# A four-layer transformer kernel whose steps are written out in one order, with the inverse root of one layer formed on VectorE

## The chip, the cores and the metric

The kernel runs on one core of a Trainium2 chip. The metric is device time in microseconds. Three runs of the kernel before took 1157.16, 1159.32 and 1162.14 us; the median is 1159.32 us. Five engines work side by side, each through its own list of instructions in a fixed order: TensorE (PE, with its weight loads as PEld), VectorE (DVE), ScalarE (ACT), GpSimd (POOL) and SyncE (SP, which here only issues DMAs). Semaphores order them.

## The reference

The input is x, 4 batches of 512 tokens of 256 numbers, and a condition vector for each batch. Four layers follow one another; every layer works on the whole of x, and batches never mix.

```python
# layer 0: one head, rmsnorm and film, softmax attention, MLP with exact gelu
h = film(rmsnorm(x)); Q, K, V = h@q_w, h@k_w, h@v_w
x = x + softmax(Q@K.T * 256**-0.5) @ V @ proj_w;  x = x + gelu(film(rmsnorm(x))@w1) @ w2
# layer 1: 16 heads of 16, layernorm, cosine attention: q and k are scaled to length 1
q = q / max(sqrt(sum(q*q)), 1e-12) * exp(min(scale_mul, log 100));  k = k / max(sqrt(sum(k*k)), 1e-12)
x = x + gamma1 * proj(softmax(q@k.T) @ v);  x = x + gamma2 * mlp(ln(x))
# layer 2: 16 heads, layernorm, softmax(q@k.T / 4), gates, MLP
# layer 3: 16 heads, softmax(q@k.T) / 16, no MLP; output = norm(h1) + h1
```

## The kernel before

One batch of one layer is a *job*; there are 16 jobs, 0 to 15. A job of layers 1 to 3 has 4 *units* of 4 heads, and a unit has 16 score steps (4 token blocks of 128 by 4 heads). Work is cut into some 2,400 *steps*, and the list `PLAN` holds them in one order. Every engine walks the whole list and does its own share of each step, so the list sets the order on each engine, on SP's DMA queue too; nothing is reordered at run time. The steps that the prediction speaks of:

- `scores` (L701): a 64-row matmul whose 128x512 result lands in one bank of PSUM; ACT reads it with an exponential into `probs` (L908 one bank, L905 two banks in one instruction, where two scores of layer 1 stand next to each other in the list and their banks too). Two such matmuls use the upper and the lower 64 rows of the array and run side by side.
- `max` (L676), in layers 2 and 3 alone: the same product of another unit the other way round; DVE reduces it to a row maximum (L1231). In layer 1 `gmax` (L684, read by DVE at L1211) gives a bound in its place.
- `av` (L714): four matmuls with 32 columns each, `probs` times V, into a bank of their own (`AVB`).
- Dense products (L602, L603, L604: three fp32r products for one exact one) for q, k, v, proj, fc1 and fc2; `oT1`, `oT2`, `hT1` and `hT2` are transposes.
- The results of all these but `av` go round a ring of 7 banks (`RING = 7`). A matmul that claims a bank waits until the reader of its last use but six is done (`claim`).
- In layer 1 `qktok` puts q and k, token by token, into `qk`; `qkss` squares (ACT) and sums (DVE, L1162); `qkroot` clamps the sums (DVE, L1167) and takes the root (ACT, L878); `qkrs` takes the reciprocal (DVE, L1171) and scales (L1173); `qknorm` multiplies (DVE, L1180); `q` and `k` then transpose `qk` (PE, L664).

`PLAN` is computed. Tables such as `COSINE` and `FFN` give steps a time in ticks (a tick is four score steps), and sorting by these gives the order in layer 0. In layers 1 to 3 the score and maximum steps stand in pairs, and for each two ticks a pattern says how they mix with the rest: in `"p6 A p8 0 p4 1"` six steps of scores and maxima come, then two `av` (`A`), eight more, the other steps of the first tick, four, and those of the second tick. All windows of a layer share eight patterns.

Of the kernel before, what the change touches and what calls it, by code (L numbers as in the profile page):

```python
# [6 lines left out]
F32R = mybir.dt.float32r  # L7
ALU = mybir.AluOpType
# [5 lines left out]
P = 128  # L14
# [13 lines left out]
EPS = (1e-6, 1e-6, 1e-5, 1e-5)  # L28
SCALE = (DIM ** -0.5, 1.0, HD ** -0.5, 1.0)
# [27 lines left out]
def direct(j):  # L57
# [29 lines left out]
LEAD_IN = {"stat1": (-24.09,), "norm1": (-23.23,), "hT1": (-14.74, -14.56), "qktok": (-12.53, -12.04, -11.51, -10.52),
           "qkss": (-12.22, -11.69, -11.15, -10.36), "qkroot": (-10.28,), "v": (-7.19, -7.01), "qkrs": (-9.94,),
           "qknorm": (-9.71, -9.63, -9.35, -9.17), "q": (-8.33, -7.97), "k": (-8.15, -7.79),
           "stack": (-7.03, -6.95, -0.36, 1.0),  # L90
           "gmax": (-5.39, -5.21, -5.03, -4.85, -4.67, -4.49, -3.6, -3.42, -2.52, -2.34, -2.16, -1.98, -1.8, -1.62, -1.44, -1.26),
           "shift1": (-0.98, -0.98), "crow": (-0.9, 0.28, 1.7, 1.7)}
COSINE = {"hT1": (-15.95, -15.04), "qktok": (-13.9, -13.8, -12.05, -11.4), "qkss": (-12.9, -12.7, -11.9, -10.95),
          "qkroot": (-10.5,), "v": (-10.95, -9.2), "qkrs": (-10.15,), "qknorm": (-9.85, -9.8, -9.65, -9.6),
          "q": (-8.9, -8.4), "k": (-8.8, -8.2), "stack": (-7.3, -6.0, -2.65, 0.6), "stat1": (-18.0,), "norm1": (-17.2,),
          "gmax": (-7.9, -7.89, -7.4, -7.39, -6.9, -6.89, -6.4, -6.39, -5.9, -5.89, -5.4, -5.39, -4.9, -4.89, -4.4, -4.39),
          "shift1": (-4.0, -4.0), "crow": (-2.99, -2.5, -1.05, 1.95)}
QKV = {"hT1": (-18.7, -14.34), "q": (-12.95, -10.7), "k": (-12.7, -10.05), "v": (-8.75, -5.2),
       "stack": (-8.25, -7.85, -2.25, 0.45), "stat1": (-22.35,), "norm1": (-20.3,)}
ATTN = {"oT1": (17.1, 17.56, 17.57, 17.83), "oT2": (18.45, 18.71), "proj": (19.2, 19.85), "stat2": (20.7,),  # L100
        "norm2": (22.55,)}
FFN = {"hT2": (23.5, 23.91), "fc1": (25.6, 25.81, 25.82, 25.83, 29.55, 29.56, 29.57, 29.58), "gelu": (25.84, 29.59),
       "fc2a": (27.45, 29.55), "fc2": (30.55, 31.2)}
FFN3 = {"hT2": (23.3, 23.76), "fc1": (25.6, 25.61, 25.72, 25.73, 29.65, 29.66, 29.67, 29.68), "gelu": (25.74, 29.69),
        "fc2a": (26.65, 27.9), "fc2": (31.15, 31.55)}
OUTPUT = {"gatefix": (20.05,), "final": (23.3, 25.45, 26.35, 31.45), "store": (27.25, 30.85, 30.95, 33.7),
          "bias": (18.35,)}
LAST = {"bias": (-0.3,), "gatefix": (14.5,), "oT1": (17.45, 17.96, 18.17, 18.48), "oT2": (19.1, 19.31),
        "proj": (19.45, 19.95), "base": (20.55, 26.35), "stat2": (20.7,), "centre": (21.65, 22.05, 24.65, 25.95),
        "final": (23.25, 26.75, 27.2, 30.2), "store": (19.6, 22.35, 22.95, 24.05)}  # L110
FOR_LAYER = {"gate": (7.7,), "gateout": (10.9,), "gatecast": (11.15, 28.25, 44.35, 56.55), "load_rows": (15.4,),
             "load_mod": (12.45, 33.55), "modrow": (29.75, 46.4), "mod": (30.95, 47.05), "load_gate": (50.6,),
             "load_qkv": (40.9, 43.2, 44.85), "split_qkv": (43.55, 45.3, 50.1), "load_wp": (7.0,), "split_wp": (8.3,),
             "load_w1": (9.9, 11.9, 17.9, 19.35), "split_w1": (10.7, 12.7, 18.7, 20.3),
             "load_w2": (13.9, 16.35, 22.15, 22.5), "split_w2": (14.45, 17.6, 23.55, 25.05)}
FOR_LAST = {"gate": (7.7,), "gateout": (11.45,), "gatecast": (14.75, 26.2, 45.15, 58.65), "load_rows": (14.7,),
            "load_wp": (2.1,), "split_wp": (4.35,), "vones": (-14.55, 3.95)}
# [18 lines left out]
def timed(table, j):  # L136

    return [(TICKS * j + at, (kind, UNITS * j + i, 0) if kind in ("stack", "crow") else (kind, j, i))
            for kind, times in table.items() for i, at in enumerate(times)]


def around(j):

# [1349 lines left out]
```

## Time and profile before

| | busy us | share of the span | instructions |
|---|---|---|---|
| PE | 1085.3 | 94% | 6697 |
| DVE | 702.5 | 61% | 1479 |
| ACT | 794.0 | 69% | 1331 |
| POOL | 490.3 | 42% | 446 |

The profiled execution took 1158.51 us; its span, from the first to the last instruction, is 1156.7 us, and the mean granted clock of TensorE is 0.985. Ends of matmuls are modelled: PE counts as busy while a matmul is in its pipeline, so a slower sequence of matmuls can show as a busy engine. The time from the start of one matmul to the start of the next tells more than the busy share. The chain of waits puts 72% of the span on PE, 9% on DVE, 8% on ACT and 4% on POOL.

### The profile page before, as it was taken

How to read it: one execution, taken by the hardware profiler on the slowest of the kernel's cores; microseconds unless marked ns; L12 is line 12 of the kernel's file. 1: busy time of each engine (PE TensorE's matmuls, PEld its weight loads, DVE VectorE, ACT ScalarE, POOL GpSimd, SP SyncE). 2: the span in 40 equal slices, each digit the busy share in tenths (PEclk: the TensorE clock that was granted, in tenths of full speed). 3: DMA queues.
4: the chain of work that ended last, by engine and by line, in shares of the span. 5: the costliest groups of instructions: out<-in, count | busy, mean ns of one | idle time of the engine just before them, and what ended most of it. 6: DMA issues, size and time to landing. Idle time of an engine off the chain costs nothing.

```text
span 1156.7 us, 19632 instructions
## 1 busy us (share of the span) xinstructions
PE 1085.3 (94%) x6697; PEld 706.0 (61%) x6697; DVE 702.5 (61%) x1479; ACT 794.0 (69%) x1331; POOL 490.3 (42%) x446
## 2 busy tenths in 40 slices
PE   8799989789899999999999999999999999999985
PEld 5577878555565656656657566666656566555442
DVE  6554446545264364234864865865865856898974
ACT  3563655477888678796686686687686787686763
POOL 2553642613633633654335453244344345254122
PEclk9999999999999999999999999999999999999998
DMA  7000001213303203221132231032121211232301
GB/s 234 18 29 28 1 20 38 52 31 101 88 28 95 54 2 90 75 64 29 28 84 65 69 102 38 2 83 65 41 71 29 52 42 52 55 84 56 84 12 36
DMA packets 36385, 64.45 MB, mean 56 GB/s; under 512 B 7208, under 2 KB 22312, under 8 KB 36288
## 3 DMA queue, kind: packets, MB, share of 16 engines
q1 hardware_dynamic: 36288, 63.20, 20.6%
q8 instruction: 56, 0.92, 0.3%
q14 instruction: 41, 0.34, 0.1%
HBM read 22.90 MB, written 2.12 MB: 22 GB/s over the span
## 4 chain that ended last, share of the span: by engine, by line
PE 72%; DVE 9%; ACT 8%; issue 5%; POOL 4%; DMA 1%; SPq 0%; POOLq 0%; DVEq 0%; ACTq 0%
PE AVB L714 13%; PE rings L602 13%; PE rings L604 11%; PE rings L603 11%; PE rings L701 10%; PE rings L676 6%; DVE m L1231 2%; ACT probs L908 2%; PE rings L754 2%; PE rings L749 2%; PE rings L645 2%; POOL gT_l L1334 1%; ACT L908 1%; PE rings L766 1%; POOL tok L1355 1%
## 5 line engine op out<-in xcount | busy, mean ns | idle before, releaser
L1231 DVE TENSOR_REDUCE m<-rings 128x1 fp32r<-128x512 f32 x512 | 319.1, 682 | 101.6 <-PE rings L676 78.4
L908 ACT ACTIVATE probs<-rings 128x512 f32<-128x512 f32 x570 | 297.3, 617 | 96.0 <-PE rings L676 84.5
L701 PE MATMUL rings<-SQ,SK 64*128 64x512 f32 x768 | 236.3, 440 | 12.5 <-ACT probs L905 4.7
L676 PE MATMUL rings<-SK,SQ 63*128 63x512 f32 x512 | 200.9, 459 | 5.4 <-ACT probs L908 4.2
L714 PE MATMUL AVB<-probs,V 128*32 128x512 f32 x1536 | 192.9, 609 | 0.6 <-issue 0.4
L701 PEld LDWEIGHTS rings<-SQ,SK 64*128 64x128 f32 x768 | 107.9, 185 | 139.1 <-issue 52.6
L1334 POOL TENSOR_TENSOR gT_l<-gT_f,gT_h 128x512 fp32r<-128x512 f32 x96 | 121.1, 1282 | 73.9 <-ACT gT_h L968 71.9
L905 ACT ACTIVATE probs<-rings 128x1024 f32<-128x1024 f32 x99 | 97.4, 1035 | 35.9 <-PE rings L701 21.9
L602 PE MATMUL rings<-w_h,gT_h 128*128 128x256 f32 x384 | 111.3, 290 | 2.8 <-POOL gT_l L1334 2.0
L676 PEld LDWEIGHTS rings<-SK,SQ 63*128 63x128 f32 x512 | 84.5, 185 | 39.6 <-ACT probs L908 33.0
L603 PE MATMUL rings<-w_l,gT_h 128*128 128x256 f32 x384 | 107.6, 280 | 0.0
L604 PE MATMUL rings<-w_h,gT_l 128*128 128x256 f32 x384 | 107.5, 280 | 0.0
L968 ACT ACTIVATE gT_f<-rings,colv 128x512 f32<-128x512 f32 x96 | 66.8, 696 | 30.1 <-PE rings L604 27.3
L714 PEld LDWEIGHTS AVB<-probs,V 128*32 128x32 f32 x1536 | 39.9, 110 | 75.8 <-issue 61.7
L602 PEld LDWEIGHTS rings<-w_h,gT_h 128*128 128x128 f32 x384 | 73.2, 191 | 14.1 <-issue 7.6
L602 PE MATMUL rings<-postT_h,w_h 128*128 128x512 f32 x192 | 78.2, 407 | 3.6 <-ACT gT_h L968 2.4
L1329 POOL TENSOR_TENSOR postT_l<-postT_f,postT_h 128x512 fp32r<-128x512 f32 x24 | 32.1, 1337 | 112.7 <-ACT postT_h L844 112.3
L1368 POOL TENSOR_TENSOR tmp<-tmp,gates 128x512 f32<-128x512 f32 x32 | 41.1, 1284 | 88.3 <-DVE tmp L1298 47.0
L604 PE MATMUL rings<-postT_h,w_l 128*128 128x512 f32 x192 | 75.4, 393 | 0.0
L603 PE MATMUL rings<-postT_l,w_h 128*128 128x512 f32 x192 | 75.3, 392 | 0.0
L1298 DVE TENSOR_TENSOR tmp<-rings,rowp 128x512 f32<-128x512 f32 x40 | 27.5, 688 | 78.4 <-PE rings L604 78.4
L1329 POOL TENSOR_TENSOR hT_l<-hT_f,hT_h 128x512 fp32r<-128x512 f32 x30 | 38.7, 1293 | 85.3 <-ACT hT_h L844 85.1
(190 smaller groups left out, 2188.6 us busy)
## 6 DMA issues: line engine op xcount, KB each, us to landing
SQ<-qh SPq DMA_DIRECT2D x96, 128.0 KB, 2.6
SK<-kh SPq DMA_DIRECT2D x96, 128.0 KB, 2.8
SQ<-ql SPq DMA_DIRECT2D x48, 128.0 KB, 2.7
SK<-kl SPq DMA_DIRECT2D x48, 128.0 KB, 2.9
raw<-in_w SPq DMA_DIRECT2D x20, 256.0 KB, 2.7
wmod_s<-in_wmod SPq DMA_DIRECT2D x6, 512.0 KB, 4.2
gates<-gate_rows SPq DMA_DIRECT2D x12, 256.0 KB, 3.4
raw<-in_wqkv SPq DMA_DIRECT2D x9, 256.0 KB, 2.7
```

Of the source, the lines that this page charges most:

```text
L602: pe.matmul(out, sh, mh, start=first, stop=False)
L603: pe.matmul(out, sh, ml, start=False, stop=False)
L604: return pe.matmul(out, sl, mh, start=False, stop=last)
L676: mm = pe.matmul(o[:, :], SQ[a % 4][r:r + KS, n // 2, c * P:(c + 1) * P], SK[a % 4][r:r + KS, n // 2, :], start=True, stop=True)
L701: mm = pe.matmul(o[:, :], SK[a % 4][r:r + KS + 1, n // 2, c * P:(c + 1) * P], SQ[a % 4][r:r + KS + 1, n // 2, :], start=True, stop=True)
L714: mm = pe.matmul(AVB[32 * n:32 * n + 32, :], V[j % 2][:, i, (HD + 1) * h:(HD + 1) * h + 32], probs[:, (4 * t + n) % PROBS, :], start=(i == ...
L905: act.activation(probs[:, n % PROBS:n % PROBS + 2, :], two_banks(kind, a, i), ACT.Exp, scale=SCALE[layer(unit_job(a))]).then_inc(done["sco ...
L908: act.activation(probs[:, n % PROBS, :], bank(kind, a, i)[:, :], ACT.Exp, scale=SCALE[layer(unit_job(a))]).then_inc(done["scores"], 1)
L968: ins = act.activation(dst[:, m % (MT // 2), :], bank("fc1", a, m)[:, :], ACT.Gelu, bias=colv[:, layer(a), col:col + 1])
L1231: nc.vector.tensor_reduce(m16[:, col:col + 1], bank(kind, a, i)[:, :], AX_X, ALU.max, negate=True).then_inc(done["max"], 1)
L1329: nc.gpsimd.tensor_tensor(lo, full, hi.bitcast(F32), ALU.subtract).then_inc(done[kind], 1)
L1334: nc.gpsimd.tensor_tensor(gT_l[:, m, :], gT_f[:, m, :], gT_h[:, m, :].bitcast(F32), ALU.subtract).then_inc(g_lo, 1)
```

## The change

Two things change.

First, the tables, the patterns and the planner go. `TURNS` now holds the order itself as a text of 17 strings: each token is a step's code with a count (`s3` is three `scores`, `a` one `av`), and `sequence` says which job and index the n-th step of a kind has. The set of steps is the same, and each kind keeps nearly its own sequence; what changes is how the kinds mix, in every layer and on every engine, SP's queue among them.

Second, in layer 1 ACT's Square root is gone, with the semaphore for it. DVE clamps the sums, makes a first guess of the inverse root from the bits of the number (one instruction that reads them as an integer), and refines it with three Newton steps of three instructions, each of which waits for the one before. The reciprocal goes. The temporary `rt` lies in a part of `tok1`.

```diff
-COSINE = {"hT1": (-15.95, -15.04), "qktok": (-13.9, -13.8, -12.05, -11.4), "qkss": (-12.9, -12.7, -11.9, -10.95),
...
-PAIR = ("p6 A p6 0 p6 1", "p4 A p6 0 p4 1", "p8 A p2 0 p8 1", "p6 A p6 0 p6 1", "p6 A p8 0 p4 1", "p6 A p8 0 p6 1", "p6 A p8 0 p4 1", "p6 A p8 0 p4 1")
...
+TURNS = (
+    "r b n lf c wq h lm h wq lq b L q wq q k2 E v2 n",
...
+    "s lp K s3 C d2 s wp s3 V K s2 Q2 Z C Q Z Q Z a s4 Z v s3 R s2 I s a2 lg a s4 N s2 N v N2 a s2 C s2 b s2 y q k "
...
+    "s m s a s m s m ld s m K a m s m s2 m o wd h ld o3 s2 t a m3 s t O q O m wd m2 s k p2 s m s2 lf m2 a m s m2 s2 "
...
+def plan_steps():
+    turn = {kind: iter(sequence(kind)) for kind in CODE.values()}
+    plan = []
+    for token in " ".join(TURNS).split():
+        code = token.rstrip("0123456789")
+        for _ in range(int(token[len(code):] or 1)):
+            plan.append((CODE[code], *next(turn[CODE[code]])))
     return plan
...
+        rt = tok1[:, 0, 0:TT * 2 * HEADS].rearrange("p (t h) -> p t h", t=TT)
...
-                elif kind == "qkroot":
-                    act.wait_ge(ss_ready, nth(kind, a))
-                    act.activation(rs[:, :, :], ss[:, :, :], ACT.Sqrt).then_inc(done[kind], 1)
...
                     if a > BATCH and i == 0:
-                        dve.wait_ge(done["qkroot"], nth("qkroot", a - 1))
+                        dve.wait_ge(done["qkrs"], nth("qkrs", a - 1))
...
-                    nc.vector.tensor_scalar(ss[:, :, :], ss[:, :, :], 1e-24, None, ALU.max).then_inc(ss_ready, 1)
+                    if nth(kind, a) > 1:
+                        dve.wait_ge(kbar_ready, CH * (nth(kind, a) - 1))
+                    link(nc.vector.tensor_scalar(ss[:, :, :], ss[:, :, :], 1e-24, None, ALU.max))
+                    nc.vector.tensor_scalar(rs[:, :, :].bitcast(I32), ss[:, :, :].bitcast(I32), -0.5, float(ROOT_GUESS),
+                                            ALU.mult, ALU.add).then_inc(done[kind], 1)
                 elif kind == "qkrs":
                     dve.wait_ge(done["qkroot"], nth("qkroot", a))
-                    link(nc.vector.reciprocal(rs[:, :, :], rs[:, :, :]))
+                    for _ in range(ROOT_STEPS):
+                        link(nc.vector.scalar_tensor_tensor(out=rt[:, :, :], in0=ss[:, :, :], scalar=-0.5, in1=rs[:, :, :],
+                                                            op0=ALU.mult, op1=ALU.mult))
+                        link(nc.vector.tensor_tensor(rt[:, :, :], rt[:, :, :], rs[:, :, :], ALU.mult))
+                        link(nc.vector.scalar_tensor_tensor(out=rs[:, :, :], in0=rt[:, :, :], scalar=1.5, in1=rs[:, :, :],
+                                                            op0=ALU.add, op1=ALU.mult))
```

Three places show how the order moves. Line numbers of the kernel after are 51 lower on PE (L714 is L663 there, L701 is L650, L676 is L625, L602 is L551). The first is PE in layer 2, behind the projection of its first batch; before, this stands there:

```order
L714 MATMUL AVB<-probs,V 32x512 x8
L701 MATMUL rings<-SQ,SK 128x512
L676 MATMUL rings<-SK,SQ 128x512
L701 MATMUL rings<-SQ,SK 128x512
L676 MATMUL rings<-SK,SQ 128x512
L701 MATMUL rings<-SQ,SK 128x512
L676 MATMUL rings<-SK,SQ 128x512
L701 MATMUL rings<-SQ,SK 128x512
L676 MATMUL rings<-SK,SQ 128x512
L602 MATMUL rings<-hT_h,wqkv_h 128x512
```

A run of eight 64-row matmuls follows two `av`, and a run of twelve stands ahead of them. Now, at the same place on PE:

```order
L663 MATMUL AVB<-probs,V 32x512 x4
L625 MATMUL rings<-SK,SQ 128x512
L650 MATMUL rings<-SQ,SK 128x512
L625 MATMUL rings<-SK,SQ 128x512 x2
L650 MATMUL rings<-SQ,SK 128x512 x2
L663 MATMUL AVB<-probs,V 32x512 x4
L650 MATMUL rings<-SQ,SK 128x512
L625 MATMUL rings<-SK,SQ 128x512
L650 MATMUL rings<-SQ,SK 128x512
L625 MATMUL rings<-SK,SQ 128x512
L663 MATMUL AVB<-probs,V 32x512 x4
```

The `av` stand singly, and the runs between them have six and four.

The second place is PE in layer 1, where q and k of its second batch are transposed (`unit,qk`); `wqkv` is the product for v. Before:

```order
L604 MATMUL rings<-wqkv_h,hT_l 128x256
L714 MATMUL AVB<-probs,V 32x512 x4
L701 MATMUL rings<-SQ,SK 128x512 x4
L664 MATMUL rings<-unit,qk 128x128 x8
L645 MATMUL rings<-unit,tok 128x128 x4
```

Now, from the `av` group behind the second product for v to the transposes:

```order
L663 MATMUL AVB<-probs,V 32x512 x4
L650 MATMUL rings<-SQ,SK 128x512 x6
L587 MATMUL rings<-wmod_s,condS 4x512 x2
L613 MATMUL rings<-unit,qk 128x128 x12
L594 MATMUL rings<-unit,tok 128x128 x4
L613 MATMUL rings<-unit,qk 128x128 x4
```

Ahead of the transposes there are now six scores in place of four, and the product for the gates, which stood behind them.

The third place is DVE in layer 0, between the k of the first batch (`kl`) and the first score reduction (`small<-rings`); `stats`, `mv` and `var` are the statistics of batch 1. Before:

```order
L1201 SCALAR_TENSOR_TENSOR kl<-rings,colv,kh 128x512 x2
L1040 TENSOR_TENSOR rowp<-rings,rowp 128x256
L1085 BN_STATS stats<-X 128x6 x4
L1088 BN_AGGR mv<-stats 128x2 x4
L1092 TENSOR_TENSOR var<-mv 128x4
L1093 TENSOR_TENSOR var<-var,mv 128x4
L1115 TENSOR_SCALAR tok_49<-X,rstd 128x256 x4
L1244 TENSOR_REDUCE small<-rings 128x1
```

Now the same statistics stand ahead of q and k:

```order
L1030 BN_STATS stats<-X 128x6 x4
L1033 BN_AGGR mv<-stats 128x2 x4
L1037 TENSOR_TENSOR var<-mv 128x4
L1038 TENSOR_TENSOR var<-var,mv 128x4
L1155 SCALAR_TENSOR_TENSOR ql<-rings,colv,qh 128x512
L991 CAST wqkv_h<-rings 128x2x256
L992 TENSOR_TENSOR wqkv_l<-rings,wqkv_h 128x2x256
L1155 SCALAR_TENSOR_TENSOR ql<-rings,colv,qh 128x512
L1155 SCALAR_TENSOR_TENSOR kl<-rings,colv,kh 128x512 x2
L948 TENSOR_REDUCE rcp<-unit 128x8
```

They moved ahead of four subtractions that wait for PE, and `rowp` moved far behind; six small instructions for constants (`headscale`, from L948 on) now stand ahead of the first score reduction.

## Rows read from the trace of the kernel before

**Rows 1.** Busy time in windows between first scores: us, engines' busy us, PEclk, DMA, GB/s.
```profile
0.00:225.10 225.10, 199.66 (x1073) 160.93 (x1073) 125.95 (x314) 107.92 (x189) 99.42 (x96) 0.98 0.17 50
225.10:308.90 83.80, 75.24 (x470) 47.50 (x470) 32.47 (x56) 64.85 (x89) 32.12 (x27) 0.98 0.27 71
634.80:719.60 84.80, 83.51 (x530) 52.91 (x530) 57.94 (x115) 63.20 (x112) 39.21 (x33) 1.00 0.25 66
968.00:1026.20 58.20, 57.60 (x371) 31.47 (x367) 52.38 (x109) 42.82 (x83) 25.60 (x29) 1.00 0.30 77
```

**Rows 2.** PE in time, a stretch of layer 2: start, duration, instruction, count.
```profile
661.78 0.39 PE L604 MATMUL rings<-hT_h,wqkv_l 128*128 128x512 f32 x1
662.10 0.50 PE L701 MATMUL rings<-SQ,SK 64*128 64x512 f32 x1
...
662.68 0.43 PE L693 MATMUL rings<-unit,m 64*16 64x64 f32 x2
663.04 1.92 PE L714 MATMUL AVB<-probs,V 128*32 128x512 f32 x16
664.89 0.50 PE L701 MATMUL rings<-SQ,SK 64*128 64x512 f32 x1
...
665.24 0.63 PE L701 MATMUL rings<-SQ,SK 64*128 64x512 f32 x2
665.47 0.39 PE L676 MATMUL rings<-SK,SQ 63*128 63x512 f32 x1
...
667.49 0.39 PE L602 MATMUL rings<-wqkv_h,hT_h 128*128 128x256 f32 x1
```

**Rows 3.** PE in time, a stretch of layer 3; brackets: idle before, and releaser.
```profile
1012.21 0.50 PE L701 MATMUL rings<-SQ,SK 64*128 64x512 f32 x1
...
1015.33 0.47 PE L701 MATMUL rings<-SQ,SK 64*128 64x512 f32 x1 [0.33 <-DVE m L1231]
...
1016.94 1.06 PE L714 MATMUL AVB<-probs,V 128*32 128x512 f32 x8
```

**Rows 4.** Costliest groups of instructions: busy us, mean ns; idle before and releaser.
```profile
L1231 DVE TENSOR_REDUCE m<-rings 128x1 fp32r<-128x512 f32 x512 | 319.1, 682 | 101.6 <-PE rings L676 78.4
L908 ACT ACTIVATE probs<-rings 128x512 f32<-128x512 f32 x570 | 297.3, 617 | 96.0 <-PE rings L676 84.5
...
L905 ACT ACTIVATE probs<-rings 128x1024 f32<-128x1024 f32 x99 | 97.4, 1035 | 35.9 <-PE rings L701 21.9
```

**Rows 5.** ACT in time at one square root of layer 1.
```profile
251.78 1.28 ACT L878 ACT_TABLE_LOAD   x1
253.08 0.31 ACT L878 ACTIVATE rs<-ss 128x128 f32<-128x128 f32 x1
253.41 1.28 ACT L905 ACT_TABLE_LOAD   x1
254.70 1.94 ACT L905 ACTIVATE probs<-rings 128x1024 f32<-128x1024 f32 x2
```

**Rows 6.** DVE in time at the same place.
```profile
251.97 0.23 DVE L1167 TENSOR_SCALAR ss<-ss 128x128 f32<-128x128 f32 x1
253.42 0.95 DVE L1171 RECIPROCAL rs<-rs 128x128 f32<-128x128 f32 x1 [1.22 <-ACT rs L878]
254.41 0.22 DVE L1173 TENSOR_TENSOR rs<-rs,rowh 128x64 f32<-128x64 f32 x1
```

**Rows 7.** PE in time at the same place.
```profile
253.00 1.06 PE L714 MATMUL AVB<-probs,V 128*32 128x512 f32 x8
253.99 0.50 PE L701 MATMUL rings<-SQ,SK 64*128 64x512 f32 x2
255.78 0.49 PE L701 MATMUL rings<-SQ,SK 64*128 64x512 f32 x2 [1.29 <-ACT probs L905]
257.31 1.06 PE L664 MATMUL rings<-unit,qk 128*128 128x128 f32 x8 [1.04 <-DVE qk L1180]
```

**Rows 8.** Chain of waits in layer 0, in order of time: start, us, what.
```profile
6.11 8.85 DMA gT_f<-in_wp
...
26.39 1.32 DVE stats L1085 x4
...
29.99 3.17 DVE tok L1115 x4
33.16 0.61 DVE small L1244
```

More of the change, by code:

```diff
@@ L87 @@
[L87 to L92, printed above, removed]
@@ L136, in timed @@
[L136 to L142, printed above, removed]
-    if not multi(j):
-        return [s for s in timed((SINGLE0, SINGLE1, SINGLE2, SINGLE3)[j], j) if s[1] not in FIRST] + timed((FFN0, FFN1, FFN2, FFN3)[j], j)
-    steps = timed(LEAD_IN, j) if j == BATCH else timed(COSINE if layer(j) == 1 else QKV if j > 2 * BATCH else {**QKV, **TO_LAYER2}, j)
-    if j == JOBS - 1:
-        return steps + timed(LAST, j)
-    return steps + timed(ATTN, j) + timed(FFN if layer(j) < LAYERS - 1 else OUTPUT, j)
@@ L165, in row_pairs @@
-def row_pairs(scores, maxima):
-    if not maxima:
-        return scores
-    return [s for n in (0, 2) for s in (scores[n], maxima[n + 1], scores[n + 1], maxima[n])]
-def in_order(pattern, pairs, av, rest):
-    out, n = [], 0
-    for what in pattern.split():
-        if what in "Aab":
-            out += av if what == "A" else av[:1] if what == "a" else av[1:]
-        elif what[0] == "p":
-            out += pairs[n:n + int(what[1:])]
-            n += int(what[1:])
-        else:
-            out += rest[int(what)]
-    return out + pairs[n:]
@@ L186, in multi_window @@
[L186 to L205 removed]
+CODE = {"s": "scores", "m": "max", "a": "av", "t": "shift", "g": "gmax", "u": "shift1", "K": "stack", "C":
[7 rows of a table added]
@@ new lines, in sequence @@
+def sequence(kind):
+    jobs, ffn, many = range(JOBS), range(JOBS - BATCH), range(BATCH, JOBS)
+    units, layers, gated = range(UNITS * BATCH, UNITS * JOBS), range(LAYERS), range(1, LAYERS)
+    places = {"scores": (units, 16), "av": (units, TT), "stack": (units, 1), "shift": (units[UNITS * BATCH:], 2),
+              "crow": (units[:UNITS * BATCH], 1), "load_gate": (gated, 1), "gate": (gated, 1), "gateout": (gated, 1),
+              "gatecast": (many, 1), "oT1": (many, TT), "oT2": (many, CH), "hT2": (ffn, CH), "fc1": (ffn, MT),
+              "gelu": (ffn, 2), "fc2a": (ffn, 2), "fc2": (ffn, 2), "norm2": (jobs[:-1], 1), "fold": (range(1), 2),
+              "headscale": (range(1, 2), 1), "base": (jobs[-1:], 2), "centre": (jobs[-1:], TT), "load_rows": (layers, 1)}
+    if kind == "max":
+        return [(u, i ^ 1) for u in units[UNITS * BATCH:] for i in range(16)]
+    if kind in ("load_mod", "modrow", "mod"):
+        return [(l, i) for l in layers for i in range(mod_rows(l))]
+    if kind in ("load_w1", "load_qkv"):
+        first = (0, 2, 3, 1) if kind == "load_w1" else (0, 2, 1)
+        return [(l, i) for l in layers for i in (sorted(first) if l else first)]
+    if kind == "bias":
+        return [(j, 0) for j in (0, 1, 2, 3, 12, 13, 15, 14)]
+    if kind == "vones":
+        return [(j, 0) for l in (1, LAYERS - 1) for j in (BATCH * l, BATCH * l + 1)]
+    if kind in ("scores0", "soft0", "pT0"):
+        return [(j, t) for j in range(BATCH) for t in range(TT)]
+    if kind in ("qktok", "qkss", "qknorm"):
+        return [(j, t) for j in many[:BATCH] for t in range(TT)]
+    if kind in ("qkroot", "qkrs", "gmax", "shift1"):
+        return [(j, i) for j in many[:BATCH] for i in range({"gmax": 16, "shift1": 2}.get(kind, 1))]
+    if kind in ("final", "store", "gatefix"):
+        return [(j, i) for j in jobs[-BATCH:] for i in range(1 if kind == "gatefix" else TT)]
+    if kind.startswith(("load", "split")) and kind not in places:
+        return [(l, i) for l in layers for i in range({"qkv": 3, "wp": 1}.get(kind.split("_")[1], 4))]
+    there, n = places.get(kind, (jobs, 1 if kind in ("stat1", "norm1", "stat2") else 2))
+    return [(a, i) for a in there for i in range(n)]
@@ L208, in mod_rows @@
 def mod_rows(l):
     return 2 if l < LAYERS - 1 else 1
[L213 to L221 removed]
+TURNS = (
[46 rows of a table added]
+    )
```

100 lines of the change are left out of this document (3 added, 97 removed), and 53 rows, old and new, of tables (CODE, FIRST, TURNS).

## The prediction

> **What bounds the kernel now.** The first view to read is the windows table, cut where each batch's first scores begin. In layer 2 PE is busy 83.51 of 84.80 us, ACT 63.20, DVE 57.94 [rows 1]: PE is the bound, and ACT and DVE have 22 to 27 us to spare. In layer 3 PE shows 57.60 of 58.20, but DVE 52.38: two engines near the limit. In layer 1 PE idles 8.6 us of 83.8 and ACT is busy 64.85; layer 0 has 25.4 us of idle PE in 225.1. By this table a new order could win little in layers 2 and 3, where idle PE is 1.3 and 0.6 us a window. So the second view is PE in time, because ends of matmuls are modelled: there the waits hide inside "busy".
>
> In layer 2 four 64-row matmuls take 662.10 to 662.68, 0.58 us. A run of twelve takes 664.89 to 667.49, 2.60 us [rows 2]. While nothing holds it, a pair needs 0.23 us (665.24 to 665.47), so twelve need 1.38 us and some 0.2 for entering and leaving: the first one follows 0.32 us after a dense product, where pairs are 0.23 apart, and four cost 0.58 where two pairs would cost 0.46. The run loses 1.0 us. In layer 3 a run of twenty takes 1012.21 to 1016.94, 4.73 us [rows 3], against 2.30 + 0.2: it loses 2.2. The reason stands in its row: idle, released by DVE's maximum. The ring has 7 banks, a reduction takes 682 ns and an exponential 617 [rows 4], PE fills two banks in 230 ns. Six results can stand unread; whatever is longer goes at the readers' pace. 1.0 us over six matmuls beyond the sixth and 2.2 over fourteen are both **0.16 us for each matmul beyond six**.
>
> **The change part by part.** The sum is made against the profiled execution, 1158.5 us, 0.1% under the median.
>
> *Long runs in layers 2 and 3.* By counting in the old order, from the window of layer 2's first batch to the last one there are 61 runs of eight or more (eight to twenty-two). Beyond the sixth they hold 158 matmuls up to and with the first window of layer 3, and 136 in the last three. At 0.16 that is 25.3 and 21.8 us. The new order has four such runs left; six is its commonest length, with single `av` between, as the first pair of order rows shows. ACT and DVE have room up to layer 3, so I take 80% there, -20. In the last three windows DVE's own work (52.38 of 58.20) leaves at most 5.8 us each; I take -9 in all. Both ends: nothing, if the waits reappear before `av` or between runs, and -47 if all go.
>
> *The price of cutting them up.* The new order has 53 more runs, 29 more in the first stretch and 26 more in the second, two fewer elsewhere. At 0.2 each: +5.8 and +5.2. And 33 more groups of `av`: two in one group take 663.04 to 664.89, 1.85 us [rows 2], a single one 253.00 to 253.99, 0.99 [rows 7]; a split costs 2 x 0.99 - 1.85 = 0.13, 20 and 14 of them +2.6 and +1.8. Net: layer 2 with the first window of layer 3 -20 + 8.4 = **-12**, the rest of layer 3 -9 + 7 = **-2**. A boundary could cost less than 0.2 (0.12, the four's 0.58 against 0.46) or more: a dense product lasts 0.39 but the next of its kind starts after 0.23, so at most 0.16 of overlap is lost at each side, 0.32 a run. For 53 runs that is +6 to +17. The Trainium skill (TensorEngine Tiling, Key Properties) speaks against the change here: a switch of tiling mode drains the array. By that rule the price would be the 0.32 end, +6 over my sum; the row shows a score starting at 662.10 before the dense product's modelled end (661.78 + 0.39 = 662.17), so a full drain isn't seen.
>
> *The square root on ACT.* Each of four jobs of layer 1 loads a table for it (1.28 us), takes the root (0.31) and loads the exponential's again (1.28) [rows 5]. In the order of ACT's functions the switches fall from 50 to 43: seven loads (the first job's return load was for gelu and stays), 9.0 us, and 1.2 us of roots. Against that, 11 of the 99 two-bank exponentials are split, each 2 x 617 - 1035 = 0.2 us [rows 4], +2.2. ACT wins 8 us in layer 1. The Trainium skill (ScalarE: Activation LUTs, What ACT_TABLE_LOAD costs) adds about 1.38 us of drain to each load of 1.283; seven would give 18.6 us of ACT. The trace has the load but no drain: the root starts at 253.08, 0.02 after the load's end.
>
> What of it is on the path shows on PE: four scores start at 253.99, the second pair waits 1.29 us for ACT, and then the transposes wait 1.04 for DVE's normalisation; 3.3 us pass where 0.58 are needed, 2.7 lost [rows 7]. Three jobs have scores around their root, 8.1 us. I take **-7**. Ends: 0 and -10.
>
> *The Newton chain on DVE.* From clamp to scale it took 251.97 to 254.63, 2.66 us [rows 6], 1.22 of it ACT's. Now it is twelve instructions that wait for each other: clamp and guess 0.23 each, nine of the steps, the scale 0.22, and gaps of 0.04. No row has the nine's form; the same shape in one operand took 0.23, and 128x512 with two (a quarter of which would do) at most 0.68 as in the reduction of rows 4, so between 0.23 and 0.68, and I take 0.25 by the nearest row: 3.4 us. The chain grows by 0.7 us (4.6 at the far end), DVE's work by some 1.5 a job, and DVE is busy 32.47 of 83.80. Cover: between the last `qktok` and the first transposed q the old order has 10 scores, 3 `av` and 2 v on PE; the new one has 21 or 22 scores, 5 or 6 `av`, and projections or gates besides. Twelve scores at 0.115 and two `av` at 0.99 are 3.4 us more alone. I cost the chain at **0**; without the cover +0.7 to +4.6 four times, 3 to 18 us. What queues behind it on DVE is `qknorm`, which needs it anyway. The new wait of `qkroot` is for the batch before, a window earlier.
>
> *The rest of layer 1.* Seven runs of eight, three of twelve, one of sixteen: 42 matmuls beyond six, 6.7 us at 0.16; the new order has none over seven. I take **-5**. The other idle there (8.6 us in its first window, part of it counted above) I credit with **-3**.
>
> *Layer 0.* Up to 15 us PE waits for a weight [rows 8], which keeps its place in SP's queue, so nothing is won. Then DVE holds the path: statistics of batch 1 from 26.39, its normalisation at 29.99, the first score reduction at 33.16. In the new order the statistics run while PE waits for the weight; 3.6 us leave the chain and six small instructions enter it, -3. The other idle PE is in pieces of 0.5 to 2 us at other hand-overs; of it I take -5. Together **-8**; ends +5 (a hand-over that now comes late) and -16.
>
> Sum: -12 - 2 - 7 + 0 - 5 - 3 - 8 = -37. 1158.5 - 37 = **1121 us**. In layer 2 what is late next is `av` behind its exponentials; in layer 3 it is DVE.
>
> **The rivals.**
>
> *Nearly all waits go.* The order gives every hand-over the room that it needs. Layer 2 -25 + 8, the end of layer 3 -17 + 7 (5.8 in each of three windows), layer 1 -25, layer 0 -16: -68, **1090 us**. For: ACT and DVE have the room in three layers. Against: DVE at 52 of 58 us.
>
> *The readers set the pace anyway.* A run of six gives each reader three results, 1.9 to 2.0 us of work, and with a single `av` PE needs 0.9 + 0.99. DVE then reads all the time and has oT, proj and the norms besides, so the wait moves to the next run. Only layer 1's -7 and layer 0's -3 stay, and half of the price of 15.4 us is paid (the other half falls into time in which PE waits anyway): -10 + 8 = -2, **1156 us**. For: DVE in layer 3. Against: dense products between the runs, some 40 us a batch in layer 2, in which both readers catch up. The Trainium skill (TensorEngine Tiling, PSUM Bottleneck) says that tiling speeds up the array but not the emptying of PSUM; by it this rival would hold in every layer, while the trace bears it out for layer 3.
>
> *Slower: the boundaries cost and win nothing.* 53 runs and 33 `av` groups are paid in full (0.32 and 0.13: 17 + 4), the late steps of the readers hold each run as before, and the Newton chain is uncovered at half its far end (+9), against -10 from ACT and layer 0. **1178 us**. It decides as soon as less than 20 of the long runs' 47 us are won back, since 17 + 4 + 9 - 10 = +20.
>
> That the change doesn't do what it says I give no chance: the order on each engine shows it, and ACT's switches are counted there.
>
> **How the numbers follow.** Forecast (1100 to 1145) 0.48; nearly all waits 0.22; the readers 0.16; slower 0.14. The range, 1084 to 1166, takes in the forecast, the readers' case and most of the one in which nearly all waits go; the slower case is left out. Within 0.5% (5.8 us, about what can be told from no change here) is 1153 to 1165: two thirds of the readers' case, 0.11. Faster by more: 0.75. Slower by more: 0.14.
>
> **What would show it.** Right: no run of scores and maxima over 1.2 us in layer 2; windows of layer 2 near 80 us and of layer 3 near 57; 43 table loads; PE without the 1.3 us idle in the scores around the normalisation; first score reduction near 30 us. Wrong: runs of six that take over 1.2 us with DVE or ACT as releaser (the readers); `av` waiting for `probs` by more than before; the transposes of qk waiting for DVE longer than 1.0 us (the chain); SP's DMAs for `stack` late, with scores waiting for a DMA, which the profile of before doesn't show among its long waits.

## The result, and the profile after

The changed kernel takes 1068.89 us (median of four runs, 1065.98 to 1071.78), the kernel before beside it 1159.81 us: ratio 0.922, 95% interval 0.918 to 0.925. The direction was right and the size was not: -91 us came where -37 was forecast, and the time lies 15 us under the range. The profiled execution of the kernel after has a span of 1065.4 us.

First the windows of the kernel after, cut at first scores: layer 0, layer 1, layer 2 with layer 3's first window, the next two, and the stretch from the last batch's first scores to PE's end; behind them the three single windows that answer to [rows 1]. Columns as in [rows 1].

```profile
0.00:206.00 206.00, 195.31 (x1083) 161.92 (x1083) 133.04 (x323) 111.04 (x192) 106.09 (x100) 0.99 0.18 55
206.00:501.70 295.70, 286.76 (x1915) 190.03 (x1914) 155.72 (x314) 242.37 (x357) 139.21 (x119) 0.98 0.26 68
501.70:891.00 389.30, 387.68 (x2612) 244.86 (x2611) 282.53 (x570) 304.63 (x542) 176.45 (x151) 1.00 0.21 55
891.00:1003.40 112.40, 111.80 (x760) 59.39 (x758) 106.45 (x213) 87.36 (x166) 52.31 (x59) 1.00 0.33 82
1003.40:1055.60 52.20, 48.78 (x338) 23.64 (x334) 36.15 (x82) 38.71 (x76) 12.58 (x18) 1.00 0.12 32
...
206.00:275.90 69.90, 69.82 (x466) 46.99 (x467) 33.72 (x66) 59.62 (x87) 31.58 (x28) 0.98 0.31 84
580.70:659.40 78.70, 78.18 (x521) 48.67 (x520) 55.66 (x112) 63.18 (x113) 40.86 (x35) 1.00 0.26 74
891.00:947.10 56.10, 55.90 (x390) 29.62 (x386) 51.98 (x108) 45.70 (x87) 29.37 (x32) 1.00 0.36 91
```

The same five stretches of the kernel before; the first is in [rows 1].

```profile
225.10:550.60 325.50, 303.06 (x1928) 192.93 (x1930) 143.20 (x285) 254.63 (x361) 144.93 (x121) 0.98 0.23 62
550.60:968.10 417.50, 411.41 (x2620) 262.10 (x2616) 283.09 (x569) 308.19 (x545) 181.10 (x153) 1.00 0.21 53
968.10:1084.70 116.60, 115.27 (x735) 62.70 (x731) 103.31 (x209) 84.14 (x163) 48.65 (x56) 1.00 0.29 74
1084.70:1146.90 62.20, 55.83 (x351) 27.39 (x350) 40.55 (x89) 39.17 (x78) 12.56 (x18) 0.95 0.10 29
```

| stretch | before | after | difference | forecast |
|---|---|---|---|---|
| layer 0 | 225.1 | 206.0 | -19 | -8 |
| layer 1 | 325.5 | 295.7 | -30 | -15 |
| layer 2, first window of layer 3 | 417.5 | 389.3 | -28 | -12 |
| next two windows | 116.6 | 112.4 | -4 | } -2 |
| last stretch | 62.2 | 52.2 | -10 | } |

ACT and DVE do the same work as before within 14 us a stretch. In layer 0 most of what went is idle time of PE (25.4 to 10.7 us, 15 of the 19). In layer 1 idle time gave 13 of the 30 us (22.4 to 8.9), and 16 left PE's "busy" time. In layer 2 and layer 3's first window idle was 6.1 and became 1.6, and the other 24 us left the "busy" time, where the forecast had looked for it.

PE in layer 2 of the kernel after, one run and what follows it (compare [rows 2]):

```profile
597.14 0.49 PE L650 MATMUL rings<-SQ,SK 64*128 64x512 f32 x1
...
597.47 0.40 PE L650 MATMUL rings<-SQ,SK 64*128 64x512 f32 x2
597.70 0.41 PE L625 MATMUL rings<-SK,SQ 63*128 63x512 f32 x2
598.04 1.06 PE L663 MATMUL AVB<-probs,V 128*32 128x512 f32 x8
599.03 0.50 PE L625 MATMUL rings<-SK,SQ 63*128 63x512 f32 x1
```

Six matmuls take 0.90 us, a single `av` 0.99. Nothing waits. The groups of [rows 4] in the kernel after:

```profile
L853 ACT ACTIVATE probs<-rings 128x512 f32<-128x512 f32 x592 | 314.2, 612 | 91.6 <-PE rings L650 49.5
L1185 DVE TENSOR_REDUCE m<-rings 128x1 fp32r<-128x512 f32 x512 | 319.2, 681 | 65.2 <-PE rings L625 39.0
```

Each read lasts as long as before (612 ns where it was 617, 681 where it was 682); only when it is asked for has changed. In layer 0 (compare [rows 8]) DVE now normalises batch 1 while PE works, and reduces the first scores 4.7 us earlier:

```profile
26.69 1.13 DVE L1060 TENSOR_SCALAR tok<-X,rstd 128x256 f32<-128x256 f32 x4
28.50 0.69 DVE L1198 TENSOR_REDUCE small<-rings 128x1 f32<-128x512 f32 x1 [0.68 <-PE rings L553]
```

### The profile page after: what moved, and what is told of

The parts are those of the page before. It is cut to its first block, busy times and chain, and to the rows that moved or that the text cites. A ratio compares the mean times of both kernels' runs of the same rounds, so it can differ in the third digit from the quotient of the medians.

```text
span 1065.4 us, 19684 instructions
## 1 busy us (share of the span) xinstructions
PE 1030.3 (97%) x6697; PEld 679.8 (64%) x6697; DVE 720.2 (68%) x1515; ACT 784.1 (74%) x1331; POOL 490.2 (46%) x446
## 4 chain that ended last, share of the span: by engine, by line
PE 83%; DVE 8%; ACT 5%; issue 2%; DMA 1%; POOL 1%; SPq 1%; POOLq 0%; DVEq 0%; ACTq 0%
PE AVB L663 15%; PE rings L551 14%; PE rings L553 13%; PE rings L552 13%; PE rings L650 10%; PE rings L625 6%; PE rings L698 3%; PE rings L594 2%; PE rings L703 2%; DVE m L1185 2%; ACT gT_h L913 1%; ACT gT_f L913 1%; PE rings L715 1%; PE rings L575 1%; DMA gT_f<-in_wp 1%
## 5 line engine op out<-in xcount | busy, mean ns | idle before, releaser
L853 ACT ACTIVATE probs<-rings 128x512 f32<-128x512 f32 x592 | 314.2, 612 | 91.6 <-PE rings L650 49.5
L650 PE MATMUL rings<-SQ,SK 64*128 64x512 f32 x768 | 200.2, 440 | 3.3 <-DMA SQ<-cT 1.0
L663 PE MATMUL AVB<-probs,V 128*32 128x512 f32 x1536 | 199.1, 602 | 0.0
L650 PEld LDWEIGHTS rings<-SQ,SK 64*128 64x128 f32 x768 | 92.5, 185 | 97.2 <-issue 35.5
L625 PE MATMUL rings<-SK,SQ 63*128 63x512 f32 x512 | 151.6, 437 | 0.7 <-ACT probs L853 0.2
L551 PE MATMUL rings<-w_h,gT_h 128*128 128x256 f32 x384 | 111.5, 290 | 3.3 <-DVE modb L976 2.7
L625 PEld LDWEIGHTS rings<-SK,SQ 63*128 63x128 f32 x512 | 70.2, 185 | 50.8 <-issue 21.1
L850 ACT ACTIVATE probs<-rings 128x1024 f32<-128x1024 f32 x88 | 86.5, 1045 | 13.0 <-issue 5.5
L551 PEld LDWEIGHTS rings<-w_h,gT_h 128*128 128x128 f32 x384 | 72.5, 189 | 16.7 <-issue 5.1
L663 PEld LDWEIGHTS AVB<-probs,V 128*32 128x32 f32 x1536 | 37.0, 108 | 71.9 <-issue 57.9
L551 PE MATMUL rings<-postT_h,w_h 128*128 128x512 f32 x192 | 78.2, 407 | 0.1
L552 PEld LDWEIGHTS rings<-w_l,gT_h 128*128 128x128 f32 x384 | 72.5, 189 | 0.3
L553 PEld LDWEIGHTS rings<-w_h,gT_l 128*128 128x128 f32 x384 | 72.5, 189 | 0.0
L913 ACT ACTIVATE gT_h<-rings,colv 128x512 fp32r<-128x512 f32 x96 | 67.2, 700 | 0.0
```

The lines of the kernel that those rows point to most:

```text
L551: pe.matmul(out, sh, mh, start=first, stop=False)
L552: pe.matmul(out, sh, ml, start=False, stop=False)
L553: return pe.matmul(out, sl, mh, start=False, stop=last)
L625: mm = pe.matmul(o[:, :], SQ[a % 4][r:r + KS, n // 2, c * P:(c + 1) * P], SK[a % 4][r:r + KS, n // 2, :], start=True, stop=True)
L650: mm = pe.matmul(o[:, :], SK[a % 4][r:r + KS + 1, n // 2, c * P:(c + 1) * P], SQ[a % 4][r:r + KS + 1, n // 2, :], start=True, stop=True)
L663: mm = pe.matmul(AVB[32 * n:32 * n + 32, :], V[j % 2][:, i, (HD + 1) * h:(HD + 1) * h + 32], probs[:, (4 * t + n) % PROBS, :], start=(i == ...
```

## The experiments

All ratios are to the kernel before, with a 95% interval. "Old order" is the list of the kernel before, "new order" that of the kernel after.

**The two halves of the change.** e1 is the kernel before with the lines of the Newton chain, e2 the kernel after with ScalarE's square root.

```diff
 # e1: kernel before            # e2: kernel after, the same lines the other way
-act.activation(rs[:, :, :], ss[:, :, :], ACT.Sqrt)
-link(nc.vector.reciprocal(rs[:, :, :], rs[:, :, :]))
+guess on DVE, then three Newton steps
```

> The old order with VectorE's Newton root in place of ScalarE's square root: part two of the change alone. Theory O (the order gives nearly all, the root little): the three stalls around the root lose their table load, 2.3 us of idle PE each, but the chain on DVE is longer and the old order has only 10 scores to cover it; 3 to 8 us faster than before, 1152 to 1157. Theory R (the root was what held layer 1, whose four windows lost 30 us): 20 us or more, 1140 or less.

> The new order with ScalarE's square root and VectorE's reciprocal as before: part one alone. Theory O: 4 to 10 us slower than the changed kernel, 1073 to 1079, with 50 table loads. Theory R: 20 us or more slower, 1089 or above.

e1: 1165.13 us, 1.005 (1.003 to 1.007), 6 us slower, where both theories had a gain. e2: 1071.45, 0.924 (0.920 to 0.928), 3 us over the kernel after, and their runs overlap. So almost all of the gain is the order. In e1 PE's transposes wait 12.4 us for the normalised q and k, in four places; before it was 3.3. In e2 they wait 0.7, but scores wait 7.5 us for exponentials in three places: the three stalls of the forecast (8.1). The chain buys those back and pays with its own: 6.5 us in the kernel after.

**Where the gain of the order lies.** Three lists joined from the two orders at a step, all with ScalarE's root.

```diff
-PLAN = old order
+PLAN = new[:cut] + [s for s in old if s not in new[:cut]]   # e3: cut at layer 1's first scores; e4: at layer 2's
+PLAN = old[:cut] + [s for s in new if s not in old[:cut]]   # e5: cut at layer 2's first scores
```

> The new order up to the first scores of layer 1, every later step in the old order, with the square root on ScalarE. Theory O: layer 0's gain is its own and is kept: first scores near 206 us in place of 225, and the whole 19 us faster, 1141. Rival (a stretch that ends sooner meets steps that are late for other reasons, and part is given back): first scores near 206, but the whole only 5 to 12 us faster, 1148 to 1155.

> The new order up to the first scores of layer 2, every later step in the old order, with the square root on ScalarE. Theory O: layer 0's 19 us and layer 1's 30 less the 4 to 10 that belong to the root: 39 to 45 us faster, 1115 to 1121; windows of layer 2 at 83 to 85 us as before. Theory R: layer 1 keeps its 83 us windows, and the whole is 19 to 25 us faster, 1135 to 1141.

> The old order up to the first scores of layer 2, every later step in the new order, square root on ScalarE. If the parts add up: layers 2 and 3 gave 42 us in the changed kernel (28 in the five windows up to layer 3's first, 4 in the next two, 10 in the last stretch), so 1115 to 1120, and first scores of layer 2 at 550 us as before. If a part of it only followed from an earlier start, 1125 to 1140.

e3 1134.13 (0.978, 0.974 to 0.982), e4 1112.01 (0.960, 0.956 to 0.964), e5 1116.45 (0.964, 0.962 to 0.967). The parts add up: -25 in layer 0, -22 more in layer 1, -42 in layers 2 and 3, 89 in all where e2 has 88. e3's layer 0 takes 202.9 us; the kernel after, with the chain, 206.0.

**Is it the length of the runs?** e6 and e9 cut the long runs by rule and keep the old order of all else; e7 makes them all long; e8 makes some long in the new order.

```diff
-plan += in_order(PAIR..., pairs, av, rest)
+plan += evenly(pairs, av, rest)   # e6: pairs dealt among the blocks [av], [av], rest 0, rest 1
+plan += spread(pairs, av, rest)   # e9: pieces of 4 or 6, evenly in PE time among single dense steps
-PAIR = ("p6 A p6 0 p6 1", ...)
+PAIR = ("p8 A 0 1",) * 8          # e7
+the first av of a pair stands beside the second, the runs around it join   # e8, new order
```

> The old order, but in layers 2 and 3 the same steps of each two ticks are dealt evenly: the two av stand singly and scores and maxima are divided among the gaps. Runs of eight and more fall from 61 to 40, matmuls beyond the sixth from 294 to 130; 65 more runs and 53 more av groups. Run theory at the predicted 0.16 us: -26 + 13 + 7 = -6 us; at the 0.21 that the runs lost by the traces: -34 + 20 = -14 us, 1145. Rival (the length of runs is not what costs, it is the place of each step): the price without the gain, 10 to 20 us slower.

> The old order, but in layers 2 and 3 every two ticks have the pattern of eight scores and maxima, two av, all other steps, and the next eight behind them: runs of 12 and 18, 550 matmuls beyond the sixth in place of 294, 41 runs fewer. Run theory at 0.16: +41 - 8 = 33 us slower; at 0.21: +54 - 8 = 46 us slower, 1205. Rival (readers set the pace however the runs are cut): within 10 us of before.

> The changed kernel, but in layers 2 and 3 the first av of a pair is put off to stand beside the second where the exponentials' buffers allow it: runs of 12 to 16 come back (76 matmuls beyond the sixth in place of 17), 15 av groups fewer. Run theory: +12 - 2 - 4 = 6 us slower than the changed kernel at 0.21, 3 at 0.16. Rival (single av cost more than they give): 4 to 6 us faster.

> The kernel before, whose planner keeps its due times; in layers 2 and 3 alone the scores and maxima of two ticks are cut into pieces of four or six, and each piece goes to the place among the dense steps and av that is nearest to an even spacing in PE time. Up to layer 3's second window no run is longer than six (40 of four, 80 of six; 22 more runs than before and 32 more av groups), behind it five of ten or twelve. The run that only dealt the pairs block by block cost 30 us. Spacing theory (readers need the results evenly in time, not only in short runs): layer 2 with layer 3's first window -35 + 5 + 4, the rest -15 + 5, so about 1123, windows of layer 2 near 78. Hand-fit theory (only the written order's own place for each step wins): 1155 to 1190, as in the run before.

e6 1188.91 (1.026, 1.022 to 1.030); e7 1284.53 (1.109, 1.106 to 1.113); e8 1077.10 (0.929, 0.926 to 0.933); e9 1207.2 (1.040, 1.037 to 1.043). Long runs do cost: e8 gives back 8 us where 6 were expected (its 58 further matmuls beyond six make 12 us at 0.21, less 4 for 11 runs and 15 `av` groups saved); e7 costs 126 us, about three times its forecast. But cutting them in the old order costs more than it wins (e6, +30 us), and so does spacing them evenly (e9, +47); both are worse than either of their theories had. In e9 the median run of six takes 0.91 us, the unblocked price, and the mean 1.25: most runs are right and a few dozen wait long. One, PE of e9 behind a gelu (start, duration, in brackets the idle before):

```profile
603.95 0.49 PE L726 MATMUL rings<-SQ,SK 64*128 64x512 f32 x1
605.60 0.49 PE L701 MATMUL rings<-SK,SQ 63*128 63x512 f32 x1 [1.15 <-ACT probs L933]
```

The second matmul waits for an exponential of the run ahead, which stands on ACT behind the gelu. The kernel before has that hand-over too; ACT, and PE at the same time:

```profile
678.20 1.28 ACT L968 ACT_TABLE_LOAD   x1 [0.26 <-PE rings L604]
...
684.24 1.28 ACT L908 ACT_TABLE_LOAD   x1
685.54 3.05 ACT L908 ACTIVATE probs<-rings 128x512 f32<-128x512 f32 x6
```

```profile
685.11 0.50 PE L701 MATMUL rings<-SQ,SK 64*128 64x512 f32 x1
686.19 0.49 PE L676 MATMUL rings<-SK,SQ 63*128 63x512 f32 x1 [0.58 <-ACT probs L908]
```

From load to load ACT is away for 7.3 us, and the scores come before it is back. In the kernel after ACT is away for 7.9 us (543.20 to 551.08, two copies of v among it), but PE has four fc1 and a v to do. The run behind them starts with five banks empty by the semaphores in the trace; the sixth comes free at 549.23, where its last matmul needs it, and the run takes 1.15 us:

```profile
543.20 1.28 ACT L913 ACT_TABLE_LOAD   x1 [0.29 <-PE rings L553]
...
549.79 1.28 ACT L853 ACT_TABLE_LOAD   x1
551.08 3.09 ACT L853 ACTIVATE probs<-rings 128x512 f32<-128x512 f32 x6
```

```profile
548.56 0.73 PE L625 MATMUL rings<-SK,SQ 63*128 63x512 f32 x4
549.13 0.64 PE L650 MATMUL rings<-SQ,SK 64*128 64x512 f32 x2
549.71 1.92 PE L663 MATMUL AVB<-probs,V 128*32 128x512 f32 x16
```

So a second theory: what counts is not six, but the banks that are empty when the run starts, dense results included. Three runs test it.

**Place, and the ring.** e12 takes a bank from the ring, e13 undoes the cover behind five gelu, e14 shifts 69 runs by one step with every length kept.

```diff
-RING = 7
+RING = 6                                                    # e12
-gelu, fc1, fc1, fc1, fc1, v, <run>
+gelu, <run>, fc1, fc1, fc1, fc1, v                          # e13, five places
-<run>, fc1, fc1, ...
+fc1, <run>, fc1, ...                                        # e14, 69 places in layers 2 and 3
```

> The kernel after with a ring of six banks in place of seven. Run theory with its threshold (PE waits 0.16 to 0.21 us for each matmul beyond the banks that can stand unread, which are now five): 115 runs of six in layers 2 and 3 lose one each, 16 of seven and more two each, so +23 to +31 there, 1092 to 1100 and more if dense blocks wait too. Rival (the runs are so far apart that the readers keep up, and the length is without meaning): under +8.

> The kernel after; at five of the ten gelu that lie in layer 2's windows the next run of scores and maxima stands directly behind gelu on PE, ahead of the two to five dense steps that stood between (the number of runs is the same; one has twelve in place of six). ACT is busy with one gelu for 7.3 us from table load to the exponential's load back. Place theory (a hand-over needs PE work while its reader is busy): five runs wait 1.5 to 4 us each, +8 to +20, 1077 to 1089, all within the first three windows of layer 2. Run theory (only the length counts): +1.3 for the run of twelve, 1070.

> The kernel after; in layers 2 and 3, 69 runs of scores and maxima that have two steps of other work behind them stand one of these steps later, so every run keeps its length, and up to layer 3 there are 16 more av groups of one (2 us by 0.13). Place theory (the written order fits every hand-over to its reader): waits come back in many places, +15 to +40, 1084 to 1109. Run theory: +2 to +4, 1071 to 1073.

e12 1155.51 (0.995, 0.993 to 0.997): one bank less takes back 87 of the 91 us. By first scores 56 of them lie in layers 2 and 3, twice what the rule "beyond the banks" gave there, and 32 in layers 0 and 1. e13 1080.72 (0.931, 0.927 to 0.934): +12, as the place theory had it, though in windows up to the fourth. e14 1149.48 (0.991, 0.988 to 0.994): +81, twice the place theory's upper end, with no run longer. PE of e12 in the same run as the six matmuls shown of the kernel after, behind the projection of layer 2's first batch:

```profile
641.35 0.50 PE L650 MATMUL rings<-SQ,SK 64*128 64x512 f32 x1
...
641.70 0.40 PE L650 MATMUL rings<-SQ,SK 64*128 64x512 f32 x2
641.93 0.77 PE L625 MATMUL rings<-SK,SQ 63*128 63x512 f32 x2
642.64 1.06 PE L663 MATMUL AVB<-probs,V 128*32 128x512 f32 x8
```

1.29 us in place of 0.90: the sixth waits for the bank of the projection, which DVE has still to read. In e14 PE, then ACT, then one window:

```profile
757.35 0.40 PE L553 MATMUL rings<-postT_h,w_l 128*128 128x512 f32 x1
757.68 0.73 PE L625 MATMUL rings<-SK,SQ 63*128 63x512 f32 x3
...
762.17 0.80 PE L551 MATMUL rings<-postT_h,w_h 128*128 128x512 f32 x1 [3.52 <-ACT gT_h L913]
762.77 0.63 PE L552 MATMUL rings<-postT_l,w_h 128*128 128x512 f32 x1
763.19 0.63 PE L553 MATMUL rings<-postT_h,w_l 128*128 128x512 f32 x1
```

```profile
759.56 1.28 ACT L913 ACT_TABLE_LOAD   x1
760.86 0.69 ACT L913 ACTIVATE gT_f<-rings,colv 128x512 f32<-128x512 f32 x1
...
765.14 0.69 ACT L913 ACTIVATE gT_f<-rings,colv 128x512 f32<-128x512 f32 x1 [3.02 <-PE rings L553]
```

```profile
762.10:765.20 3.10, 3.03 (x7) 2.45 (x8) 0.00 (x0) 0.08 (x2) 1.27 (x1) 0.51 0.00 0
```

One fc1 is done, six results of the run fill the other banks, and the second fc1 needs the bank of the first, which gelu has to read behind two exponentials and a table load. PE stands for 3.5 us, then ACT for 3.0, since gelu now needs the second fc1. Behind that idle the granted clock is 0.51, the lower of its two levels (1.2 and 2.4 GHz), and products of the same form start 0.43 us apart in place of 0.23 until 765. Nine such places lose 3.3 to 3.8 us each, and behind each of them the clock is at the lower level (0.50 or 0.51) for 3.4 us or more; slow products and the second wait come on top. In layers 2 and 3 the old order has no such wait at a block of fc1, so e14 shows that place alone can cost this much, and not that the old order lost its time at these places.

**The length of the chain.** e11 has six Newton steps; e10 gives the first batch of layer 1 its square root on ACT back; e15 is e10 with two Newton steps (its root is good to some five parts in a million).

```diff
-ROOT_GUESS, ROOT_STEPS = 0x5F3759DF, 3
+ROOT_GUESS, ROOT_STEPS = 0x5F3759DF, 6                      # e11;  2 in e15
+if a == BATCH: ss_ready -> act.activation(rs, ss, ACT.Sqrt) -> nc.vector.reciprocal(rs, rs)   # e10, e15
```

> The kernel after with six Newton steps in place of three: nine more dependent instructions of 0.29 + 0.04 us in each of four chains, 3.0 us a chain. Prediction's theory (scores and av on PE cover the chain in the last three batches; the first has no cover): +3, 1072. Rival (the chain is on the path each time): +12, 1081. Covered everywhere: 1069.

> The kernel after, but the first batch of layer 1, whose root falls into layer 0's end, takes ScalarE's square root and DVE's reciprocal again; the other three keep the Newton chain. Theory (in layer 0's end the chain and the normalisation behind it run beside GpSimd's 128x512 products and last 1.2 to 1.3 us an instruction, and PE waits 2.6 us for q and k): layer 0's window falls from 206.0 to about 202.5, layer 1's stay, 1065 to 1066. Rival (the first table loads back push the first scores' exponentials): layer 1's first window gives back 3 us or more, 1069 or over.

> The kernel of e10 (ScalarE's root for the first batch of layer 1, the Newton chain for the other three) with two Newton steps in place of three; the root is then good to some five parts in a million in place of single precision. By the slope of six steps (11 us for nine instructions in four chains, 0.3 each) three instructions fewer in three chains give -2.8: 1059. If the chain is covered: 1062.

e11 1079.97 (0.930, 0.928 to 0.933): +11; with nine instructions more the transposes wait in every batch. The wait of the transposes in layers 0 and 1 (us in all, times, longest), of the kernel after and of e11:

```profile
PE rings L613 <- DVE qk L1134: 6.5, 3, 2.6
```

```profile
PE rings L613 <- DVE qk L1134: 16.2, 4, 5.4
```

e10 1062.13 (0.915, 0.913 to 0.918) and e15 1058.36 (0.911, 0.907 to 0.915): both beat both kernels. e10's layer 0 takes 202.0 us in place of 206.0, and its layer 1 keeps the chain's gain (291.8 in four windows; 303.8 with the root on ACT throughout, e2). So the chain is worth 9 us against e2 where it is used in the last three batches alone, and 13 with two steps.

## Why the prediction was wrong

54 us are missing: 28 in layers 2 and 3, 15 in layer 1 and 11 in layer 0.

**The long runs, -20 and -9: the step that failed.** The forecast took 0.16 us for each matmul beyond the sixth from two runs, and let 80% and 40% of it go. Each run's time in the trace, less what it needs unblocked, puts the loss of runs of eight or more at 37.4 us up to layer 3's first window (158 matmuls, 0.24 each) and 23.9 behind it (136, 0.18); 3.2 us of these 61 are left in the kernel after. So the term was mis-sized twice: the loss was 61 us and not 47, and 95% of it went, not 62% (in the last three windows, where DVE was to leave 9, it was 20.7 of 23.9). And the cause was not the length alone. "Six" is the ring when all else in it has been read. Of the 93 runs of the old order up to layer 3's second window, 55 were longer than the banks empty at their start, and these lost 41.7 us; the other 38 nothing. In e6, whose runs are shorter, some 60 of 134 were, and lost 46.2. In the kernel after some 65 of 123 are, but most by a bank or two that comes free while the run goes on: 6.7 us. The forecast had both ingredients in its rows (ACT's and DVE's other reads share the ring) and used only the length. By e14 the same lengths one step later lose more than layers 2 and 3 had gained, so their 42 us hang on the place of each run as well as on its length. How they divide was not settled: e8 puts 8 us on length, e13 12 us on five places.

**The price of boundaries, +15.4: right.** A run of six takes 0.90 us, 0.21 over its three pairs, and a single `av` 0.99; at these prices the added runs and groups of layers 2 and 3 cost 15 us. The Trainium skill (TensorEngine Tiling, Key Properties) has a change of tiling mode drain the array. By the forecast's estimate that would be 0.32 a run, 1.01 for a run of six; the 0.90 doesn't show it.

**The rest of layer 1 and layer 0, -8 and -8: far too small.** e3 and e4 put 25 us of layer 0 and 22 of layer 1 on the order alone. In layer 1 all scores of a run go to one reader, ACT, and its runs of eight and more lost 17.0 us, not the 6.7 that 0.16 a matmul gave; none are left. The other idle of layer 1, and that of layer 0 but for the 3 us of DVE's statistics, the forecast had as idle PE without a reason for each piece; some 60% of the idle went in both layers. In layer 0 PE's longest waits went: for ACT's `sq` (4.6 us, now 0.7), for gelu (4.4) and for a maximum of layer 1's bound (2.4). No run takes these pieces one by one, so what each gave stays open.

The last stretch has the last part of the 136 matmuls, but the -9 left next to nothing for it. It gave 10: its runs lost 10.9 us and lose 2.9, and its granted clock rose from 0.95 to 1.00.

**The square root, -7: right** (e2 waits 7.5 us there). **The Newton chain, 0: wrong.** Its price was: left alone its instructions cost nearly what was estimated (0.29 where 0.25 was taken), and the one chain that is left alone, the second, takes 3.69 us and PE does not wait. But the first, third and fourth take 4.68, 6.72 and 6.79, since DVE's instructions are held beside POOL's products, seven of 48 in all; there PE waits 2.6, 2.3 and 1.7 us. The cover that the forecast counted is there in the last three batches: a chain less its wait is 4.4 and 5.1 us in the third and fourth, and 5.7 in e11's second (6.62, wait 0.93). In the first batch no scores stand around the chain. Of e11's 36 more instructions of 0.33 (11.9 us) 11 come through. DVE of the kernel after in the first and the fourth chain, and POOL beside them:

```profile
168.01 1.23 DVE L1114 TENSOR_SCALAR ss<-ss 128x128 f32<-128x128 f32 x1
...
174.71 3.76 DVE L1134 TENSOR_TENSOR qk<-qk,rs 128x512 f32<-128x512 f32 x3
...
373.56 1.31 DVE L1115 TENSOR_SCALAR rs<-ss 128x128 int32<-128x128 int32 x1
374.91 1.27 DVE L1121 SCALAR_TENSOR_TENSOR tok<-ss,rs 128x128 f32<-128x128 f32 x1
376.21 1.32 DVE L1123 TENSOR_TENSOR tok<-tok,rs 128x128 f32<-128x128 f32 x1
```

```profile
167.86 1.30 POOL L1277 TENSOR_TENSOR wqkv_l<-raw,wqkv_h 128x512 fp32r<-128x512 f32 x1 [6.71 <-ACT wqkv_h L767]
174.35 1.29 POOL L1283 TENSOR_TENSOR postT_l<-postT_f,postT_h 128x512 fp32r<-128x512 f32 x1 [5.20 <-ACT postT_h L793]
176.31 1.60 POOL L1283 TENSOR_TENSOR postT_l<-postT_f,postT_h 128x512 fp32r<-128x512 f32 x1 [0.67 <-ACT postT_h L793]
...
373.51 1.28 POOL L1329 TENSOR_TENSOR X<-X,tmp 128x512 f32<-128x512 f32 x1
374.75 1.28 POOL L1322 TENSOR_TENSOR tmp<-tmp,gates 128x512 f32<-128x512 f32 x1
376.11 1.28 POOL L1329 TENSOR_TENSOR X<-X,tmp 128x512 f32<-128x512 f32 x1
```

The clamp takes 1.23 us beside a POOL product and not 0.23, and three normalisations 3.76 where the form needs 0.69 each; in the fourth chain three instructions end one after another as POOL's products end. In each of the three chains DVE is held for about 3 us, longer than PE waits. By these rows POOL's products are the step that the forecast missed; no run moves them away, so it is read from the trace and not shown by a change. The Trainium skill has the rule (SBUF — State Buffer, SBUF: two separate sides): DVE, with two SBUF inputs or in a two-port mode, and GpSimd take turns on one port pair, a whole instruction at a time. The rows agree in time; that the clamp and the guess, which have one SBUF input, run in a two-port mode no row shows.

**The signs.** 43 table loads, as counted (50 before). First score reduction at 28.5 (near 30). Layer 2's windows 74 to 79 (80 forecast), layer 3's 56 (57). Five of layer 2's runs still take over 1.2 us, where none was forecast; 36 did before. The transposes wait 2.6 us for DVE, the sign against the chain. `av` waits for `probs` as before. SP's new order gave nothing of its own: PE's waits for DMAs are 1.1 us before and 2.8 after. Of the rivals "nearly all waits go" was nearest, in the sum and in each layer. Its 1090 was high because it took the long runs' loss at 47 us and layer 1's and layer 0's gain at 25 and 16.

## What to carry to other kernels

When a ring of buffers is shared, count for each burst the buffers that are empty when it starts, all readers' arrears included, and not the burst's length alone. Give PE independent work behind every instruction that takes a reader away for long (here a gelu, 7.3 us). Look for such waits in the starts of the matmuls, since a busy share can hide them. Here the order gave 88 us and the arithmetic some 3, which the scatter of the runs covers; before a chain of short instructions on DVE is called free, look at what POOL does beside it.

## What the runs showed of the hardware

- DVE instructions of 0.23 to 0.29 us lasted 1.2 to 1.3 beside a 128x512 product on POOL (seven of the 48 of the four chains); a chain that was left alone took 3.69 us, one with three of them held 6.72.
- Behind each of nine idle stretches of PE of 3.3 to 3.8 us the granted clock was at its lower level, 0.50 or 0.51 (e14): a wait costs its length and then the slower products behind it.
- One PSUM bank of seven was worth 87 us (e12), with the order unchanged and eight of the 88 two-bank exponentials split.
